# Query pieces of half a row and one-partition maxima in a two-layer transformer kernel

## What is computed

```python
x = x + _L0_xattn_ref(_layernorm(x), ctx, ctx, ...)   # gated attention, 4 heads
x = x + _L0_ffn_ref(_layernorm(x), w_gate, w_up, w_down)   # quantized
x = x + _L1_xattn_ref(_layernorm(x), ctx, ctx, ...)   # softmax attention, 16 heads of 16
x = x + _L1_ffn_ref(_layernorm(x), w_router, wi, wo)  # 8 experts, top 2, capacity 160
```

```python
def act_qdq(x):
    scale = jnp.maximum(jnp.max(jnp.abs(x)) / 32767.0, 1e-12)
    return jnp.clip(jnp.round(x / scale), -32768.0, 32767.0) * scale
```

```python
q = proj(query, w_q, b_q); k = proj(key, w_k, b_k); v = proj(value, w_v, b_v)
scores = jnp.einsum('bhqd,bhkd->bhqk', q, k) / np.sqrt(D_K)
attn = jax.nn.softmax(scores, axis=-1)
out = jnp.einsum('bsd,ed->bse', attn_times_v, w_o) + b_o
```

## Time and profile before

| | us |
|---|---|
| three executions | 600.31, 601.71, 602.09 |
| median of these | 601.71 |
| profiled execution | 600.69, its span 599.0 |
| TensorE busy | 513.8 (86% of the span) |
| VectorE busy | 376.5 (63%) |
| ScalarE busy | 317.3 (53%) |
| granted TensorE clock, mean | 0.953 of full speed |

### The profile page before, as it was taken

One profiled execution on the slowest core, in us unless ns is written; L12 is line 12 of the kernel. 1 busy time (PEld: TensorE's weight loads), 2 busy tenths in 40 slices (PEclk: granted clock), 3 DMA queues, 4 the chain that ended last, 5 costly groups with the idle time before them and its releaser, 6 DMA issues.

```text
span 599.0 us, 9299 instructions
## 1 busy us (share of the span) xinstructions
PE 513.8 (86%) x3283; PEld 362.7 (61%) x3283; DVE 376.5 (63%) x937; ACT 317.3 (53%) x654; POOL 152.6 (25%) x218
## 2 busy tenths in 40 slices
PE   0869999899999700899989999996799999999994
PEld 0548866644444300787657687874667776777773
DVE  6765689945489989788688699987403432143101
ACT  1527658823389969781388899984222112211220
POOL 2716525000000000000323133111234354434531
PEclk9979999999999955999999999999699999999998
DMA  7900000000000000025000001015133536353410
GB/s 227 308 4 2 1 2 1 2 0 1 0 0 0 1 1 0 1 77 205 1 1 2 21 18 37 2 37 176 28 110 120 185 119 204 116 184 119 134 44 22
DMA packets 31994, 37.58 MB, mean 63 GB/s; under 512 B 8656, under 2 KB 27728, under 8 KB 31952
## 3 DMA queue, kind: packets, MB, share of 16 engines
q1 hardware_dynamic: 28880, 29.07, 15.0%
q0 software_dynamic: 3072, 7.95, 4.6%
HBM read 30.14 MB, written 6.88 MB: 62 GB/s over the span
## 4 chain that ended last, share of the span: by engine, by line
PE 68%; DVE 16%; ACT 10%; issue 2%; DMA 2%; SPq 1%; POOLq 0%; POOL 0%; DVEq 0%
PE pA L2043 12%; PE pB L2061 9%; PE pC L1712 6%; PE pC L1751 5%; PE pA L1745 3%; PE pB L1761 3%; ACT arena L609 3%; PE pA L1667 2%; PE pC L1575 2%; PE pC L1667 2%; PE pB L1667 2%; ACT XIT L706 2%; PE pC L2054 2%; DVE am L1168 2%; PE pB L1841 2%
## 5 line engine op out<-in xcount | busy, mean ns | idle before, releaser
L487 POOL TENSOR_TENSOR arena<-KT,par 128x256 f32<-128x256 f32 x32 | 18.9, 613 | 248.3 <-DVE XIT L1242 186.4
L2043 PE MATMUL pA<-arena 128*128 128x320 f32 x256 | 74.1, 438 | 0.4 <-ACT arena L882 0.4
L894 ACT ACTIVATE arena<-pA 128x320 f32<-128x320 f32 x64 | 28.0, 437 | 71.9 <-PE pA L2043 71.2
L2061 PE MATMUL pB<-arena 128*128 128x256 f32 x256 | 59.3, 385 | 0.0
L2043 PEld LDWEIGHTS pA<-arena 128*128 128x128 f32 x256 | 47.4, 190 | 18.9 <-issue 1.1
L2061 PEld LDWEIGHTS pB<-arena 128*128 128x128 f32 x256 | 47.4, 190 | 9.4 <-issue 3.1
L1134 DVE TENSOR_REDUCE am<-arena 128x1 f32<-128x512 f32 x48 | 32.1, 681 | 23.0 <-ACT arena L646 22.9
L1712 PE MATMUL pC<-wdnT,XIT 128*128 128x256 f32 x192 | 42.9, 381 | 1.8 <-DVE XIT L1242 1.8
L1318 DVE TENSOR_REDUCE rm<-pA 128x16 f32<-128x2048 f32 x16 | 36.7, 2291 | 8.7 <-PE pA L1745 8.7
L1712 PEld LDWEIGHTS pC<-wdnT,XIT 128*128 128x128 f32 x192 | 36.0, 190 | 7.9 <-DVE XIT L1242 2.8
L523 POOL DMA_INDIRECT out<-arena,token x24 | 23.5, 978 | 55.0 <-DVE arena L1466 43.9
(11 more groups left out here) (342 smaller groups left out, 1156.5 us busy)
## 6 DMA issues: line engine op xcount, KB each, us to landing
arena<-in_L_ffn_wi SPq DMA_DIRECT2D x8, 1024.0 KB, 5.4
arena<-in_L_ffn_wo SPq DMA_DIRECT2D x8, 1024.0 KB
X<-in_x SPq DMA_DIRECT2D x4, 512.0 KB, 5.7
arena<-in_ctx SPq DMA_DIRECT2D x4, 512.0 KB, 5.9
out<-X SPq DMA_DIRECT2D x4, 512.0 KB, 2.9
token_rows<-arena SPq DMA_DIRECT2D x4, 512.0 KB, 5.5
arena<-in_L_ffn_w_up SPq DMA_DIRECT2D x1, 768.0 KB, 9.1
arena<-in_L_ffn_w_gate SPq DMA_DIRECT2D x1, 768.0 KB, 10.2
```

What stands on the lines that cost most here:

```text
L894: nc.scalar.activation(HT[:, u, f, :], ps[2 + f % 2][:, 0:ROWS], ACT.Relu).then_inc(s["h_relu"], 1)
L2043: last = mm(ps[2 + f % 2][:, 0:ROWS], WI[:, u, k, f * P:(f + 1) * P], XET[:, u, k, :], start=(k == 0), stop=(k == KD - 1))
L2061: last = mm(ps[4 + c][:, 0:D], HT[:, u, f, c * P:(c + 1) * P], WO[:, u, f, :], start=(f == 0), stop=(f == NFT - 1))
```

## The change

Two things change.

First, the queries of rows 12 to 15 are no longer made by two `c_query` in turn 4 but by eight `query_piece(n)`, one in each of the turns 4 to 11. Piece n makes row 12 + n // 2, feature half n % 2: two products of 128 columns into a quarter of bank 4. Each has a `piece_out(n)` on ScalarE in the next turn, ahead of `at_copy`, which waits for the piece and for the `a_turn` behind it. `scores1` of rows 12 to 15 waits for its own row's two pieces. The waits of `a_turn(2)` and `turn_2(4)` for `q_out` go.

Second, in the maxima the n columns of `gm` are transposed one by one onto one partition, side by side in n x 128 columns. One reduction gives the n maxima in `gr[0:1, 0:n]`, and `max_spread` takes these directly, with one row of `ones`. The diagonal `gd` and its instruction go.

```diff
-        QUERY_BANK = ((2, 3), (6, 7), (4, 4), (4, 6))
+        QUERY_BANK = ((2, 3), (6, 7), (4, 4))
+
+        PIECE_STEP = 4
...
+            def piece_out(n):
+                b, e = 12 + n // 2, n % 2
+                act.wait_ge(s["c_q"], 7 + n)
+
+                act.wait_ge(s["a_tr"], PIECE_STEP + n - 1)
+                nc.scalar.activation(XITv[:, e, b * P:(b + 1) * P], ps[4][:, 2 * P:3 * P], ACT.Identity, scale=0.25, bias=bq[:, e:e + 1]).then_inc(s["qt_ready"], 1)
...
+                if PIECE_STEP < t <= PIECE_STEP + 8:
+                    piece_out(t - PIECE_STEP - 1)
                 if a >= 0 and a < NB:
                     at_copy(a, a % 2)
...
-                if t == 5:
-                    q_out(3, 1)
...
-                if t == 4:
-                    q_out(3, 0)
...
                 dve.wait_ge(s["gmT"], k + 1)
-                link(V_.tensor_reduce(gr[0:n, 1:2], ps[5 if k == 3 else 0][0:n, 0:P], AX.X, ALU.max))
-                V_.tensor_scalar(gd[0:n, 0:n], ident[0:n, 0:n], gr[0:n, 1:2], None, ALU.mult).then_inc(s["gr_ready"], 1)
+
+                V_.tensor_reduce(gr[0:1, 0:n], ps[5 if k == 3 else 0][0:1, 0:n * P].rearrange("p (c n) -> p c n", c=n), AX.X, ALU.max).then_inc(s["gr_ready"], 1)
...
-                tr(ps[5 if k == 3 else 0][0:n, 0:P], gm[:, 0:n], ident[:, :]).then_inc(s["gmT"], 1)
+                for c in range(n):
+                    last = tr(ps[5 if k == 3 else 0][0:1, c * P:(c + 1) * P], gm[:, c:c + 1], ident[:, :])
+                last.then_inc(s["gmT"], 1)
...
-                mm(ps[5 if k == 3 else 0][:, 256:256 + n], ones[0:n, :], gd[0:n, 0:n], start=True, stop=True).then_inc(s["gm_all"], 1)
+                mm(ps[5 if k == 3 else 0][:, 256:256 + n], ones[0:1, :], gr[0:1, 0:n], start=True, stop=True).then_inc(s["gm_all"], 1)
...
+            def query_piece(n):
+
+                b, e = 12 + n // 2, n % 2
+                pe.wait_ge(s["c_xt"], 7 + n // 4)
+                pe.wait_ge(s["x3_ready"], PIECE_STEP + n - 2)
+                for k in range(KD):
+                    last = mm(ps[4][:, 2 * P:3 * P], wT[0][:, k, e * P:(e + 1) * P], XC4[1][:, k, (b - 12) * P:(b - 11) * P], start=(k == 0), stop=(k == KD - 1))
+                last.then_inc(s["c_q"], 1)
...
-                pe.wait_ge(s["qt_ready"], 2 * (b // 4) + 2)
+                pe.wait_ge(s["qt_ready"], 2 * (b // 4) + 2 if b < 12 else 2 * b - 16)
...
-                if b == 4:
-                    pe.wait_ge(s["qt_ready"], 8)
...
-                if t == 4:
-                    pe.wait_ge(s["x3_ready"], 2)
-                    c_query(3, 0)
-                    pe.wait_ge(s["pt_ready"], 16)
-                    c_query(3, 1)
+                if PIECE_STEP <= t < PIECE_STEP + 8:
+                    query_piece(t - PIECE_STEP)
```

More of the change, by code:

```diff
@@ L250, in build @@
         gr = sb("gr", [2, 2])
-        gd = sb("gd", [2, 2])
         sc = sb("sc", [P, 32])
@@ L1830, in a_turn @@
                     pe.wait_ge(s["pt_ready"], 4 * NB)
-                if b in (0, 2):
-                    pe.wait_ge(s["qt_ready"], 6 if b == 0 else 7)
+                if b == 0:
+                    pe.wait_ge(s["qt_ready"], 6)
                 for k in range(KD):
```

## The result

The changed kernel takes 603.37 us (median of 13 executions, 601.71 to 604.75) against 601.75 for the kernel before (13 executions, 599.69 to 604.5). The medians are 1.6 us apart. The ratio is 1.003, with a 95% interval from 1.0018 to 1.0043: by it the change costs some 1.8 us, from 1.1 to 2.6.

The account below looks back on a forecast made before the run. Each attention turn was taken as a ring through TensorE and ScalarE. Pieces 3.78 plus copies 2.0 minus 4.36 gave +1.4 us, maxima -0.36: about +1.05 on 601.2, so 602.3 us, range 600.1 to 604.6.

Parts of the forecast that it names:

- a closed ring through TensorE and ScalarE: Attention turn: TensorE from scores to second transposes, ScalarE's copies and exponentials, then scores; anything put in lengthens the 5.86 us.
- the heavy turn: Turn 4 of the second layer's attention loop, with two query products: 10.22 us against 5.86 for a plain turn.
- the base: Time of the kernel before to which the change was added: 601.2 us, the middle of four executions.
- What goes: Turn 4: the two query products, ScalarE's two copies of 512 columns and their waits; gives back 4.36 us.
- What comes on TensorE: Turns 4 to 11: eight pieces between first transposes and output transpose, all exposed, 0.47 us each, 3.78 together.
- The rule on narrow matmuls: Skill's figures of 81 ns at 128 columns, 131 at 512: pieces 2.5 times as dear, 8.5 us instead of 3.78.
- The rival that loads stand in line: Pieces' weight loads not hidden behind earlier work: 0.76 us a piece, +3.4 us, 604.6; chance 0.17 for 603 to 604.6.
- What comes on ScalarE: Eight copies of 128 columns ahead of the first PT copy, taken as exposed: 0.25 us each, 2.0 together.
- The turn: Length of an attention turn with a piece: 5.86 + 0.47 + 0.25 = 6.58 us.
- The maxima: Four global maxima, each losing a VectorE instruction: first and fourth -0.23 us, second 0, third +0.1; together -0.36.
- The sum: Queries +1.4 us and maxima -0.36: about +1.05 us, 602.3 us in all.
- the slower rival: Weight loads of pieces standing in line; turns over 6.7 us, +3.4 us, 604.6; chance 0.17 for 603 to 604.6.

Follow-up runs that it names:

- the kernel without the last group: Kernel before without the last group of query products and their two copies; turn 4 took 5.87 us against 10.22; 597.80 us in one execution against 601.30.
- the pieces alone: Changed kernel with the maxima of before, so only the query pieces are new; 603.43 us against 601.27 for the kernel before, ratio 1.0032.
- the pieces twice: Changed kernel with each piece's two products made twice; a turn with a piece took 7.07 us; 605.61 us in one execution against 601.30 for the kernel before.
- the maxima alone: Kernel before with only the change of the maxima, queries staying in turn 4; 600.94 us against 601.27, ratio 0.9994.

## Why the prediction was right, and what was off

The mechanism held: a closed ring through TensorE and ScalarE, in which the heavy turn is given back and each piece and each copy is paid for. The sizes of two terms and the base were off.

**What goes.** 4.36 us, read from the windows as the heavy turn less a plain one. Confirmed to 0.01 by the kernel without the last group.

**What comes on TensorE.** 0.47 a piece was forecast, from rows of 16 products in layer 0; 0.44 to 0.45 was measured, and all of it exposed, as turn 3 had shown. Here the estimate was 0.2 us too high over eight pieces: the 1.89 us that it divided by 16 hold one longer step of 0.21 behind the first record, and the others were 0.112 each, which gives 0.45.

**The rule on narrow matmuls.** The Trainium skill, TensorE: Matmul & The Clock Gate, section Back-to-back issue gap, gives figures from which the prediction's estimate made narrow products 2.5 times as dear by the column. Here a piece's 128 columns took 0.11 us a record, nearly the same as 128 columns of a wide product (0.107). For these products in single precision the trace disagrees, and the measurement decides. A weight load took 0.19 us here too, longer than the 0.11 from record to record, so the loads overlap each other and the products. The rival that loads stand in line falls with it: the step of a second piece is 0.44.

**What comes on ScalarE.** The reasoning held, step by step: the 0.17 us of wait for the values doesn't help, since the first PT copy ahead of it has no slack, and the copy is exposed. The size was off: 0.25 was forecast, 0.32 measured, that is 0.26 of pitch, and some 0.06 that the trace puts at the copy's waits. The prediction had looked at the piece's waits on TensorE and not at the copy's on ScalarE. Over eight turns this is +0.6 us.

That the first PT copy has no slack is true, but by little. In turn 3 of the kernel before, four more transposes ahead of the values gave ScalarE time:

```profile
322.65 0.59 ACT L779 ACTIVATE arena<-pC 128x512 f32<-128x512 f32 x1
...
322.70 1.08 PE L1761 MATMUL pB<-arena,V 128*32 128x128 f32 x32
323.71 1.09 PE L1751 MATMUL pC<-ident,arena 128*128 128x128 f32 x8
```

Here the copy ends at 323.24, 0.47 us before the second transposes start, and they still follow the values' start by 1.01 us, against 1.04 in a plain turn. So the copy holds up a plain turn by some 0.03 us, and the values' own time on TensorE is the next bound. A copy put ahead costs its full pitch, but on this reading a faster PT copy would give back no more than 0.03.

**The turn.** 6.58 forecast, 6.63 measured, and 6.74 once. That one, turn 9, is 0.11 longer at the same place in three kernels (the changed one, the pieces alone, the pieces twice) and in none of the others; there ScalarE starts the copy of the output transpose 0.36 behind the piece's copy instead of 0.27. What it waits for there isn't known.

**The maxima.** -0.23, 0, +0.1, -0.23 forecast; -0.24, 0, +0.10, -0.24 measured. That the second is hidden behind half an up product, and that the third becomes longer, could both be read ahead. The time of the maxima alone (ratio 0.9994) is too small to confirm the sum; the trace does.

**The sum.** +1.05 forecast, +1.52 by the trace, +1.8 (1.1 to 2.6) by the time. Of the missing 0.47, the copies give 0.6, turn 9 gives 0.1 and the pieces -0.2. The time of 603.37 is 1.07 above the forecast of 602.3, and 0.55 of that is the base: it was taken as 601.2, the middle of four executions, and the median of 13 is 601.75. The chances were put at 0.64 for a change within 0.3% and 0.29 for slower; the ratio of 1.003 stands on that border. That the time of 603.37 lies in the range owes something to its width, 4.5 us from 600.1 to 604.6; the turn of 6.63, against 6.58 forecast and over 6.7 for the slower rival, is the better support.

## What to carry to other kernels

To spread a block of work over several turns gains nothing when every turn is a closed ring without slack: the work is paid for in each, and small steps add copies and waits of their own. What decides is not how small a piece is but where it stands. Moved behind the first PT copy, the copy cost 0 instead of 0.32 us. With the piece moved to the one place where TensorE waited, and the copy between the exponentials, both together cost 0.26 instead of 0.77. Look for the idle time in each engine's own turn first, and check the instruction just ahead of it: a wait of 0.17 us doesn't shelter work that is put ahead of another step on which a third party waits.

## What the runs showed of the hardware

- From one ACTIVATE out of PSUM to the next it is 0.26 to 0.27 us for 128 columns with a bias, 0.26 to 0.28 for 256 columns without and 0.48 for 512 without (starts at 343.86, 344.13, 344.39 and 344.87 in the changed kernel, 344.73 and 345.01 before).
- An ACTIVATE whose late wait stood as a semaphore instruction of its own ahead of it started 0.10 us behind the end of what it waited for; one whose late wait stood on itself, 0.04. That is read from two traces and was not tested.
- On VectorE a reduction of 256 values on one partition takes 0.41 us, of 128 values on one or on two partitions 0.28.
- At 0.50 of the clock, two transposes of a single column followed one another after 0.17 us (the third maximum), not 0.23 as full products do (14 in 3.22 us); at 1.00 no pair was seen.
- The same kernel can have 59.0 or 62.9 us at the lower clock level on average in one set of executions and the next. That went with about 1.1 us of time, estimated from 0.27 us for each microsecond over 51 executions of the kernel before, and it is more than half of the effect that was to be measured; the turns in the trace didn't move by 0.01.
